# Score pass of a graph attention layer: the two edge products of a step on the two row halves of TensorE, each into a bank of its own, and the query products issued one step ahead

## The chip, the cores and the metric

The kernel runs on one core of one Trainium2 chip. The metric is the device time of one execution in microseconds. Every number of a profile below comes from one profiled execution of the kernel.

## The reference, cut to what matters

6250 nodes with 256 features go through a graph attention layer over 100,000 edges, a linear-attention block and a mixture of eight feed-forward experts. The change is in the score part of the graph attention (8 heads of 32 features):

```
k = (xn @ Wk.T + bk);  v = (xn @ Wv.T + bv);  q = (xn @ Wq.T + bq)
e = edge_attr @ We.T                      # 64 attributes -> 256, one row an edge
k_e = k[src] + e;  v_e = v[src] + e
alpha = einsum('ehc,ehc->eh', q[dst], k_e) / sqrt(32)
```

The softmax over the edges of each destination and the weighted sum of `v_e` come in later passes. The edges are sorted by destination.

## The kernel before, in words

The kernel has four stages in time: a pass over the nodes that makes the tables (to about 340 us), the **score pass** (about 340 to 1930 us), a value pass (about 2040 to 2580 us) and the expert stage (to the end). The change touches the score pass alone.

The score pass makes 450 steps (25 blocks `b` of `SB = 18`, `k = b * SB + s`). A step takes one pair of edge tiles, 2 x 125 edges, `w = 0, 1`, together with one tile of 125 nodes. The order on each engine is written out by hand and held together by semaphores:

- **SyncE** (SPq), for step `k`: loads two short rows for a later step (`load_ab`, L476), stores the finished value rows of step `k - 6` to `ve_d` (`store_ve`, L481) and loads the attributes of the 250 edges, transposed, into slot `s % 6` of the ring `att_b` (L502). A slot is free when `e_done` of six steps earlier is in. The attribute matrix `attr_t` lies in memory as 64 rows of 100,000 numbers.
- **GpSimd**, step `k`: two gathers (L625) fetch key and value rows (2 KB an edge) of 125 source nodes each into slot `s % 6` of `kg`, once the indices are copied (`idx_ready`) and the slot's last store has landed.
- **ScalarE**, step `k`: copies the indices (`start_edges`, L1060) and then makes the one-hot matrix `hott` from the spread destinations (`one_hot`, L1066 and L1067), in a ring of three.
- **TensorE**, step `k`: `qprod` (L762) for step `k - 5`, one-hot times the node tile's queries, two products into bank `2 + s % 2`; `eproj` (L746) for step `k - 5`, the edge product `attr @ We.T`, `w = 0` and `w = 1` into the two halves of bank `s % 2`; between the two, `spread` (L754) for step `k - 2`, a bf16 product on partitions 64 to 127, where `coef` and `ab_b` lie; and after these a piece of the linear-attention block (`mix`, L774 to L826; none to eight product pairs, by `mix_at`, `late_at`, `last_at`). The edge products stand on partitions 0 to 63, where `att_b` and `we` lie.
- **VectorE**, step `k`: `add_edges` (L1427) adds the edge product to keys and values of the gathered rows, `multiply` (L1435) multiplies the keys with the queries, `total` (L1441) sums over each head for step `k - 1`, `keep` (L1450) stores the sums for step `k - 2`; some steps carry a piece of the linear-attention block too.

`e_done`, `kv_added`, `q_done` and `mult_done` count the steps. `eproj` of step `k` waits until `kv_added` reaches `k - 1`, so the add of step `k - 2` has read the bank that is written again, and TensorE may be one edge product ahead. `qprod` waits in the same way for `mult_done`.

A product of fp32 operands shows as two passes in the trace: each has a weight load (PEld) and a matmul (PE), so that `eproj` has four matmul records a step.

## Time and profile before

| | |
|---|---|
| median of 3 runs | 3518.64 us (3511.38 to 3543.4) |
| profiled execution, its own time | 3552.69 us |
| its span, first to last instruction | 3550.9 us |
| mean granted TensorE clock in it | 0.961 of 2.4 GHz |
| step of the score pass, 600 to 1400 us | 226 steps in 800 us |

The span leaves out 1.8 us at the ends of the execution. The profiled execution is 34 us (1.0%) longer than the median of the runs. A busy share is the time in which an engine had an instruction in work; for DMA it is the mean over the core's 16 DMA engines of the time that their packets took.

### The profile page before, as it was taken

What the parts mean: (1) busy time and instruction counts of PE and PEld (TensorE: products, weight loads), DVE (VectorE), ACT (ScalarE), POOL (GpSimd) and SP (SyncE); (2) the same over time, 40 slices, a digit from 0 to 9 for tenths busy, and PEclk for the clock granted to TensorE, in tenths of its full rate; (3) what the DMA queues carried; (4) which work ended last, traced back from release to release, by engine and by line L of the source; (5) the groups of instructions that cost most, each with busy time, mean ns of one, the idle gap of its engine ahead of it and who ended that gap; (6) DMA issues with size and microseconds to landing.
All of it is one profiled execution on the core that took longest, in us unless ns stands there. A gap on an engine that the chain in (4) does not pass through costs nothing.

```text
span 3550.9 us, 72164 instructions
## 1 busy us (share of the span) xinstructions
PE 3186.8 (90%) x17312; PEld 2479.1 (70%) x17312; DVE 2793.7 (79%) x5687; ACT 1682.8 (47%) x4460; POOL 1646.0 (46%) x1803
## 2 busy tenths in 40 slices
PE   4997999999999999999999188888769999999999
PEld 3776666666666666666666155555569999999998
DVE  6775888888888888888887889999846666666665
ACT  1222333333333343333333256666546777777776
POOL 1223777777777777777775077777600000000000
PEclk9998899999999999999999599999979999999999
DMA  7345999899989899999998267777600000000000
GB/s 178 116 119 156 251 256 254 248 254 261 257 247 253 248 264 261 260 256 255 266 255 223 92 200 231 232 230 231 194 4 19 12 13 16 12 17 12 13 15 9
DMA packets 520909, 593.53 MB, mean 167 GB/s; under 512 B 187937, under 2 KB 396979, under 8 KB 520319
## 3 DMA queue, kind: packets, MB, share of 16 engines
q1 hardware_dynamic: 312408, 351.02, 34.0%
q0 software_dynamic: 201888, 232.77, 25.1%
q10 hardware_dynamic: 6409, 7.46, 0.7%
q8 instruction: 75, 1.23, 0.2%
q14 instruction: 129, 1.05, 0.1%
HBM read 426.91 MB, written 163.17 MB: 166 GB/s over the span
## 4 chain that ended last, share of the span: by engine, by line
PE 62%; DVE 12%; issue 8%; DMA 7%; SPq 3%; DVEq 3%; another core or an unknown queue 2%; ACT 1%; POOL 1%; ACTq 0%; POOLq 0%
PE psum L684 10%; PE psum L686 10%; PE psum L685 10%; PE psum L903 8%; PE psum L762 7%; PE psum L746 7%; PE psum L826 3%; DMA weights<-kv_tab,idx 3%; PE psum L817 2%; DVEq L1616 2%; DVE weights L1427 2%; DVE region_s L1613 1%; DVE part L1441 1%; DMA ve_d<-weights 1%
## 5 line engine op out<-in xcount | busy, mean ns | idle before, releaser
L625 POOL DMA_INDIRECT weights<-kv_tab,idx x450 | 549.1, 1220 | 254.5 <-issue 150.1
L762 PE MATMUL psum<-region_x,weights 125*125 x1800 | 493.3, 397 | 72.8 <-issue 39.7
L1183 ACT ACTIVATE region_s<-psum,bns 128x250 f32<-128x250 f32 x800 | 402.9, 554 | 287.8 <-PE psum L686 287.8
L746 PE MATMUL psum<-we,weights 64*125 64x256 f32 x1800 | 525.4, 410 | 0.0
L1665 DVE TENSOR_TENSOR parts_h<-region_s,parts_h 128x500 fp32r<-128x500 f32 x400 | 269.8, 679 | 311.2 <-ACT parts_h L1187 283.7
L903 PE MATMUL psum<-region_s 125*125 125x264 f32 x1800 | 452.5, 401 | 68.0 <-DVE region_s L1613 68.0
L1066 ACT ACTIVATE weights<-psum,region_s 125x250 f32<-125x250 f32 x450 | 211.3, 470 | 609.8 <-PE psum L754 289.0
L903 PEld LDWEIGHTS psum<-region_s 125*125 125x125 f32 x1800 | 304.6, 188 | 215.7 <-issue 76.9
L762 PEld LDWEIGHTS psum<-region_x,weights 125*125 125x125 f32 x1800 | 325.2, 191 | 177.3 <-issue 136.0
L625 POOL DMA_INDIRECT kv_more<-kv_tab,idx x300 | 370.4, 1235 | 126.9 <-issue 84.7
L746 PEld LDWEIGHTS psum<-we,weights 64*125 64x125 f32 x1800 | 298.5, 186 | 183.0 <-issue 155.2
L1427 DVE TENSOR_TENSOR weights<-weights,psum 125x1024 f32<-125x1024 f32 x225 | 274.1, 1218 | 82.7 <-remote 30.2
L1613 DVE TENSOR_TENSOR region_s<-region_s 125x512 f32<-125x512 f32 x450 | 308.5, 686 | 0.5 <-issue 0.5
L664 POOL TENSOR_SCALAR region_s<-iota,region_s 125x125 f32<-125x125 f32 x300 | 280.1, 944 | 14.7
L684 PE MATMUL psum<-parts_x,wx_up 128*128 128x250 f32 x800 | 233.9, 292 | 25.9 <-DVE wx_low L1657 25.9
L1187 ACT CAST parts_h<-region_s 128x500 fp32r<-128x500 f32 x400 | 244.2, 611 | 15.1
L817 PE MATMUL psum<-region_s,weights 128*128 128x250 f32 x800 | 225.8, 406 | 6.8 <-issue 2.9
L684 PE MATMUL psum<-wx_up,parts_h 128*125 128x256 f32 x800 | 226.8, 283 | 1.8 <-DVE region_s L1695 1.8
L1602 DVE TENSOR_TENSOR region_x<-region_x,psum 125x264 f32 x450 | 190.6, 423 | 46.9 <-issue 43.8
L686 PE MATMUL psum<-parts_x,wx_low 128*128 128x250 f32 x800 | 226.6, 283 | 0.0
L685 PE MATMUL psum<-parts_x,wx_up 128*128 128x250 f32 x800 | 226.3, 283 | 0.0
L686 PE MATMUL psum<-wx_up,parts_h 128*125 128x256 f32 x800 | 225.9, 282 | 0.0
(247 smaller groups left out, 7515.0 us busy)
## 6 DMA issues: line engine op xcount, KB each, us to landing
region_s<-ve_d SPq DMA_DIRECT2D x450, 256.0 KB, 3.0
ve_d<-weights SPq DMA_DIRECT2D x225, 256.0 KB
ve_d<-kv_more SPq DMA_DIRECT2D x150, 256.0 KB
weights<-in_attr_t SPq DMA_DIRECT2D x450, 62.5 KB
ve_d<-region_r SPq DMA_DIRECT2D x75, 256.0 KB
kv_tab<-region_s SPq DMA_DIRECT2D x50, 224.0 KB
region_s<-ab_d SPq DMA_DIRECT2D x450, 1.0 KB
weights<-kv_tab,idx POOLq DMA_INDIRECT x450
```

Source lines behind the costliest of these rows:

```text
L625: nc.gpsimd.indirect_dma_start(kg[r][0:T, w, :], None, kv_tab, bass.IndirectOffsetOnAxis(idx[:, r, w:w + 1], 0)).then_inc(gathered[r], 16)
L664: compared = nc.gpsimd.tensor_scalar(hot[:, s, w, :], iota[:, :], place_in[:, s, w:w + 1], None, ALU.is_equal)
L684: mm(to, lhs[0], rhs[0], start=start, stop=False)
L685: mm(to, lhs[0], rhs[1], start=False, stop=False)
L686: return mm(to, lhs[1], rhs[0], start=False, stop=stop)
L746: last = mm(psum[0:T, s % 2, w * D:(w + 1) * D], att_b[:, s % RP, w * T:(w + 1) * T], we[:, :], start=True, stop=True)
L762: last = mm(psum[0:T, 2 + s % 2, w * D:(w + 1) * D], hott[:, s % RA, w * T:(w + 1) * T], q_all[:, bass.ds(j, 1), :].rearrange("p o d -> p ...
L817: last = mm(psum[:, 5 if pair == 0 else 6, o * BN:(o + 1) * BN], wm1[:, c, n * 128:(n + 1) * 128], mx1t[:, c, :], start=(c == 0), stop=(c ...
L903: last = mm(bank, hot[:, s, w, :], pv[:, s, w, 0:PV], start=(w == 0), stop=(w == 1))
L1183: last = fn(fh[:, layer, o, :], psum[:, bk + e % 2, o * BN:(o + 1) * BN], ACT.Relu, bias=bns[:, layer, 1, col:col + 1], scale=bns[:, layer ...
L1427: tt(rows4, rows4, psum[0:T, s % 2, :].rearrange("p (w d) -> p w d", w=2).unsqueeze(2).broadcast_to((T, 2, 2, D)), ALU.add).then_inc(kv_ad ...
L1613: tt(pv[:, s, :, 0:D].rearrange("p w (h c) -> p w h c", h=H), vg[0:T, s].rearrange("p w (h c) -> p w h c", h=H), pv[:, s, :, D:PV].unsquee ...
```

## The change

What it does:

- `eproj` puts the two edge products of a step on different partitions: `w = 0` with attributes and weights on partitions 0 to 63, `w = 1` on 64 to 127. Each writes a bank of its own, 0 and 1, the same two in every step. It now waits until `kv_added` reaches `k`.
- `we` is held twice, once on each half of the partitions (one more constant load).
- The attribute load of a step writes 128 partitions of 125 numbers where it wrote 64 partitions of 250. Its source is walked as 2 x 64 x 125 (`w` outermost).
- `spread` goes behind both edge products, and its operands (`coef`, `ab_b`) move to partitions 0 to 63.
- `qprod` comes last of the three and is issued for step `k - 4`; the register that names its node tile is loaded one place further.

```
-        we = sb("we", [ED, D])
+        we = sb("we", [2 * ED, D])
-        ab_b = carve(8200, RP * E2 // 2).bitcast(BF16).rearrange("p (r n) -> p r n", r=RP)[64:128]
-        coef = weights[64:128, 1600:1600 + 64].bitcast(BF16)[:, 0:T]
+        ab_b = carve(8200, RP * E2 // 2).bitcast(BF16).rearrange("p (r n) -> p r n", r=RP)[0:64]
+        coef = weights[0:64, 1600:1600 + 64].bitcast(BF16)[:, 0:T]
-        att_b = weights[0:ED, 0:RP * E2].rearrange("p (r t) -> p r t", r=RP)
+        att_b = weights[:, 0:RP * T].rearrange("p (r t) -> p r t", r=RP)
-            sp.dma_start(we[:, :], a["w_e"]).then_inc(c_b, 16)
+            for w in range(2):
+                sp.dma_start(we[w * ED:(w + 1) * ED, :], a["w_e"]).then_inc(c_b, 16)
-                    sp.dma_start(att_b[:, s % RP, :], a["attr_t"][:, bass.ds(i * E2, E2)]).then_inc(att_in[s % RP], 16)
+                    sp.dma_start(att_b[:, s % RP, :], a["attr_t"][:, bass.ds(i * E2, E2)].rearrange("p (w t) -> w p t", w=2)).then_inc(att_in[s % RP], 16)
-            def eproj(k, s, turn_of, w):
-                if w == 0:
-                    pe.wait_ge(att_in[s % RP], turn_of * 16)
-                    wait(pe, kv_added, k - 1)
-                last = mm(psum[0:T, s % 2, w * D:(w + 1) * D], att_b[:, s % RP, w * T:(w + 1) * T], we[:, :], start=True, stop=True)
-                if w == 1:
-                    last.then_inc(e_done, 1)
+            def eproj(k, s, turn_of):
+                pe.wait_ge(att_in[s % RP], turn_of * 16)
+                wait(pe, kv_added, k)
+                for w in range(2):
+                    half = slice(w * ED, (w + 1) * ED)
+                    last = mm(psum[0:T, w, 0:D], att_b[half, s % RP, :], we[half, :], start=True, stop=True)
+                last.then_inc(e_done, 1)
...
-                        pe.load(regs, walk[0:1, 1, bass.ds(k, SU)])
-                    some = s >= LAGQ or not (isinstance(b, int) and b == 0)
-                    if some:
-                        qprod(k - LAGQ, (s - LAGQ) % SB, regs[s % SU])
-                        eproj(k - LAGQ, (s - LAGQ) % SB, b * (SB // RP) + (s - LAGQ) // RP + 1, 0)
+                        pe.load(regs, walk[0:1, 1, bass.ds(k + 1, SU)])
+                    if s >= LAGQ or not (isinstance(b, int) and b == 0):
+                        eproj(k - LAGQ, (s - LAGQ) % SB, b * (SB // RP) + (s - LAGQ) // RP + 1)
                     if s >= LAGS or not (isinstance(b, int) and b == 0):
                         spread(k - LAGS, (s - LAGS) % SB, b * (SB // RP) + (s - LAGS) // RP + 1)
-                    if some:
-                        eproj(k - LAGQ, (s - LAGQ) % SB, b * (SB // RP) + (s - LAGQ) // RP + 1, 1)
+                    if s >= LAGQ - 1 or not (isinstance(b, int) and b == 0):
+                        qprod(k - LAGQ + 1, (s - LAGQ + 1) % SB, regs[s % SU])
...
-                tt(rows4, rows4, psum[0:T, s % 2, :].rearrange("p (w d) -> p w d", w=2).unsqueeze(2).broadcast_to((T, 2, 2, D)),
+                tt(rows4, rows4, psum[0:T, 0:2, 0:D].unsqueeze(2).broadcast_to((T, 2, 2, D)),
```

## Rows read from the trace of the kernel before

**Rows 1.** The page: busy sums, the DMA share in 40 slices, the attribute load's row.

```profile
PE 3186.8 (90%) x17312; PEld 2479.1 (70%) x17312; DVE 2793.7 (79%) x5687; ACT 1682.8 (47%) x4460; POOL 1646.0 (46%) x1803
...
DMA  7345999899989899999998267777600000000000
...
weights<-in_attr_t SPq DMA_DIRECT2D x450, 62.5 KB
```

**Rows 2.** Busy time by stretch: us, PE, PEld, DVE, ACT, POOL, clock, DMA share, GB/s.

```profile
600.00:1400.00 800.00, 756.03 (x3237) 510.90 (x3236) 688.27 (x1205) 308.84 (x867) 578.92 (x501) 0.98 0.93 254
```

**Rows 3.** Groups of instructions with shapes, 600 to 1400 us.

```profile
L625 POOL DMA_INDIRECT weights<-kv_tab,idx x225 | 274.9, 1222 | 122.2 <-issue 70.1 <-ACT idx L1060 40.4 <-DMA ve_d<-weights 10.2
L746 PE MATMUL psum<-we,weights 64*125 64x256 f32 x902 | 262.4, 409 | 0.0
L762 PE MATMUL psum<-region_x,weights 125*125 x901 | 246.5, 396 | 35.7 <-issue 21.4 <-DVE weights L1435 6.8 <-DVE kv_more L1435 2.3
...
L1427 DVE TENSOR_TENSOR weights<-weights,psum 125x1024 f32<-125x1024 f32 x114 | 138.9, 1218 | 45.3 <-remote 15.8 <-DMA weights<-kv_tab,idx 11.0 <-PE psum L746 10.1
...
L754 PE MATMUL psum<-region_s,weights 64*125 64x250 bf16 x226 | 71.8, 318 | 8.3 <-issue 5.9 <-ACT weights L1067 2.0
```

**Rows 4.** Line L1427 (`add_edges`), 600 to 1400 us: its engine idle before it, until.

```profile
  remote: 23.8, 19
  PE psum L746: 14.3, 11
  issue: 12.4, 24
```

**Rows 5.** DMA queues and issues, 600 to 1400 us: packets, MB, share of 16 engines.

```profile
q0 software_dynamic: 101040, 115.99, 55.2%
q1 hardware_dynamic: 90519, 83.28, 35.7%
...
ve_d<-weights SPq DMA_DIRECT2D x114, 256.0 KB
ve_d<-kv_more SPq DMA_DIRECT2D x74, 256.0 KB
weights<-in_attr_t SPq DMA_DIRECT2D x226, 62.5 KB
ve_d<-region_r SPq DMA_DIRECT2D x38, 256.0 KB
region_s<-ab_d SPq DMA_DIRECT2D x226, 1.0 KB
region_s<-xnt_d SPq DMA_DIRECT2D x13, 250.0 KB
...
region_s<-skip_d SPq DMA_DIRECT2D x12, 224.0 KB
region_r<-xn_d SPq DMA_DIRECT2D x12, 224.0 KB
...
region_s<-skip_d SPq DMA_DIRECT2D x12, 26.0 KB
region_r<-xn_d SPq DMA_DIRECT2D x12, 26.0 KB
```

**Rows 6.** Timeline of TensorE in one step: start, length, what.

```profile
1013.44 0.48 PE L746 MATMUL psum<-we,weights 64*125 64x256 f32 x1
1013.45 0.32 PE L754 MATMUL psum<-region_s,weights 64*125 64x250 bf16 x1
1013.76 0.81 PE L746 MATMUL psum<-we,weights 64*125 64x256 f32 x3
```

**Rows 7.** Busy time by stretch: the load of the expert weights (SyncE's queue alone).

```profile
2000.00:2020.00 20.00, 0.00 (x0) 0.00 (x0) 19.96 (x2) 0.00 (x0) 0.00 (x0) 0.50 0.93 302
```

More of the change, by code:

```diff
@@ L337, in build @@
         f_stored = [sem(f"f_stored{u}") for u in range(2)]
-        CONST_A, CONST_B = 16 * 7, 16 * 9
+        CONST_A, CONST_B = 16 * 7, 16 * 10
         block = ctx.enter_context(nc.Block())
@@ L859, in _ @@
             each(NB, b_body)
-            pe.load(regs, walk[0:1, 1, STEPS:STEPS + SU])
+            pe.load(regs, walk[0:1, 1, STEPS + 1:STEPS + 1 + SU])
             for s in range(LAGQ):
-                qprod(STEPS - LAGQ + s, SB - LAGQ + s, regs[s])
-                eproj(STEPS - LAGQ + s, SB - LAGQ + s, (STEPS - LAGQ + s) // RP + 1, 0)
+                eproj(STEPS - LAGQ + s, SB - LAGQ + s, (STEPS - LAGQ + s) // RP + 1)
                 if s < LAGS:
                     spread(STEPS - LAGS + s, SB - LAGS + s, (STEPS - LAGS + s) // RP + 1)
-                eproj(STEPS - LAGQ + s, SB - LAGQ + s, (STEPS - LAGQ + s) // RP + 1, 1)
+                if s < LAGQ - 1:
+                    qprod(STEPS - LAGQ + 1 + s, SB - LAGQ + 1 + s, regs[s])
                 if s in last_at:
```

## The prediction

> **What bounds the kernel now.** I read the page first. TensorE has the largest busy sum, and the digits of the DMA engines stand at 8 and 9 in tenths through the score pass [rows 1]. The pass has 450 steps, one attribute load each [rows 1]. The table by stretch gives the middle of it: TensorE busy 756 of 800 us, VectorE 688, GpSimd 579, the DMA engines 0.93 at 254 GB/s, TensorE's clock 0.98 [rows 2]. With 226 steps in it a step takes 800 / 226 = 3.54 us. So four resources are within a few per cent of each other, and no one of them alone sets the step.
>
> TensorE's 95% are partly waiting time in disguise, since a record of a matmul overlaps the next: 902 records of L746 with 409 ns each would be 369 us, and they fill 262 [rows 3]. What the change wants to shorten is seen from the reader of the edge product: in front of `add_edges` VectorE waited 14.3 us for L746 in 226 steps, and 23.8 us for a releaser that the profile doesn't name [rows 4]. That is 0.06 and 0.11 us a step. The DMA engines have 7% left, 0.25 us a step. Whatever lets TensorE run faster can give no more than that before the transfers set the step.
>
> **The change, part by part.** *Edge products on two row halves.* Four passes of L746 a step. In the timeline three of them take 0.81 us, of which the last stands alone for 0.376, so a pass costs (0.81 - 0.376) / 2 = 0.22 us [rows 6] (0.376 is the median record of that line, the 0.48 of the first pass holds the wait for its weights). `spread` starts 0.01 us after the first pass, on the other half, and costs nothing now [rows 6]. If the halves run together, two passes remain in the time of four: 0.43 us less. `spread` then stands behind the edge products on the same half and must be paid: between nothing and its record of 0.32 us; I take half a pass, 0.11, as it has as many columns as a pass of L746 and only one pass. Net 0.1 to 0.4 us of TensorE's step, my value 0.3.
>
> Here a rule speaks against the change. In rows 6 `spread`, third in program order, ends at 1013.77, and the first pass of L746 at 1013.92: products on different row halves don't end in program order. The Trainium skill (TensorE: Matmul & The Clock Gate, Part 3) says that matmuls on different row groups overlap, but start and end strictly in program order. By that rule the second pass of `w = 0` would hold back the first of `w = 1`, three passes would remain, and TensorE would save 0.1 us. The trace doesn't agree with it. Neither value enters the sum below.
>
> *One pair of banks, `kv_added` up to `k`.* TensorE can't be a step ahead with the edge product any more. Behind the waiting `eproj` stand `spread`, on which ScalarE's one-hot waits and with it the indices and the gathers, `qprod` and the linear-attention piece. VectorE needs the next edge product only after multiply, total and keep, so the wait is covered while these last longer than `eproj`. If not, the cost is of the size of today's waits for L746: 0.06 us a step, 0.17 with the unnamed ones [rows 4], 30 to 80 us in all; the other bound is nothing. *`qprod` later and a step ahead:* its wait is for a product made a whole step before its use; nothing either way. *Constant load, register place:* once per kernel, nothing.
>
> *The attribute load.* This is the part that decides. It moves the same 62.5 KB [rows 5], but in 128 pieces of 500 B where there were 64 of 1000 B, and its source has the dimension of two outermost. How many DMA engines share a transfer can be counted. Each transfer gives one packet a row, and I assume one small closing packet for each engine that took part. In rows 5 the rows of the SyncE transfers are 226 x 256 stores, 226 x 64 attributes, 226 x 2 short rows, 13 x 256, and 24 x 250 for the last four: 82,100. The queue shows 90,519 packets, so 8,419 closed a transfer. With 16 engines for every one of the 739 transfers it would be 11,824; with two for the 226 two-row loads and 13 for the 24 loads of 26 KB (13 rows) it is 8,588, within 2% of the count. So a transfer is not spread over more engines than its outermost dimension gives, and I expect that of the new load: two engines, 64 pieces each, in every step, the same two.
>
> That the source's dimension counts, though the target has 128 partitions, no row shows: in every transfer of rows 5 the two sides have the same outermost size, or both a multiple of 16. The Trainium skill (DMA: Bandwidth & Descriptors, "Why a DMA increments its semaphore by 16 and not by 1") says that the engines are the largest number up to 16 that divides the slowest dimension of both sides, and its table of advice names an outermost dimension under 16 as what confines the whole transfer. The count in rows 5 agrees with it.
>
> The sum for one of these two engines, a step:
> - What it carries today: 0.93 x 3.54 = 3.29 us, less its sixteenth of the attribute load. The queue's 35.7% of 16 x 800 us are 4570 us for 83.28 MB, 18.2 GB/s [rows 5]; 64,000 B at that are 3.5 us, a sixteenth is 0.22. Leaves 3.07 us. Lower bound: all bytes, 254 GB/s x 800 us / 226 = 0.90 MB [rows 2] less 0.064, a sixteenth 52 KB, at the fastest rate that I found, 302 / 0.93 / 16 = 20.3 GB/s [rows 7]: 2.6 us.
> - Its half of the new load: 64 pieces of 500 B. By bytes at 18.2 GB/s 1.76 us; by packets, 4570 us / 90,519 = 50 ns each [rows 5], 3.2 us. I take 1.9, near the bytes, since the mean packet of that queue has 920 B.
> - Together 4.2 us (2.6 + 1.6 at 20.3 GB/s) to 6.3 us. My value: 2.8 for the old part, because the other fourteen engines will stand idle a third of the time and contend less, plus 1.9 is 4.7; at 96% use, little above today's 93%, 4.9 us.
>
> Gathers and stores need all sixteen engines to end, so the two slow ones set every step: nothing runs beside it to hide it. 450 x (4.9 - 3.54) = +612 us. Against the profiled execution that is 3552.7 + 612 = 4165 us; the median is 34 us below it, so **4130 us**. TensorE's 0.3 us drop out, as it waits. Its clock may fall in the pauses (it was 0.50 where TensorE had nothing to do, rows 7); a step's 756 / 226 = 3.35 us at full clock [rows 2] would be up to 6.7 at half, so stretches of it can add some tens of us.
>
> The bounds: 4.2 us a step gives 3519 + 450 x 0.66 = 3815; 6.3 gives 4760.
>
> **The rivals.**
> - *The load is spread over sixteen engines, and TensorE's gain comes through: faster.* For it: the target has 128 partitions, and rows 5 can't rule out that these count. Then TensorE saves 0.3 us, VectorE loses most of 0.17 us of waits [rows 4]; the DMA share caps the gain at 0.25 us. I take 0.1: 3519 - 45 = 3475 us. It decides from the point where the load's pieces cost no more than before. Against it: GpSimd's and the DMA's shares [rows 2, 3].
> - *Spread over sixteen, and nothing moves:* the transfers hold the step at 3.54 us, 3519 us, within 1%. The 500 B pieces by bytes cost what they did.
> - *Spread over sixteen, and the smaller pieces cost by the packet:* 64 more at 50 ns over 16 engines are 0.20 us a step at a share of 0.93: up to +90 us, with or without the single-bank wait (+30 to +80). 3580 us.
>
> **How the numbers follow.** Two engines 0.74, faster 0.10, unchanged 0.08, slightly slower 0.08. The likeliest case has its own range of 3815 to 4550; I give a tenth of it to more than 4550. To leave out no more than two in ten the range must reach down over the unchanged case, to 3490; above it ends at 4550. Faster by over 1%: 0.10. Within 1%, which is about what a measurement of this kernel can tell from no change: 0.09. Slower: 0.81.
>
> **What would show it.** In the changed profile a step of 4.9 us; the DMA share as a mean of 16 near 0.7 and under 200 GB/s in the score pass, though the pass is slower; q1's packets up by 64 a step for the attributes and down by 14 closing ones; L746 or `add_edges` waiting for the attribute load or for gathers, no longer for TensorE; TensorE's busy time well under 90% and a clock under 1 there. The stages behind unchanged. On TensorE the two halves' passes starting together would show the 0.43 us, three passes in a row the rule above. The prediction is wrong if q1 has 16 closing packets for each attribute load: then the step stays between 3.3 and 3.75 us and one of the rivals holds. It is wrong in size if the pieces of 500 B cost nearer 27 or nearer 50 ns than my 30.

## The result, and the profile after

The changed kernel is slower: 3822.38 us in the median of its runs (3812.48 to 3837.45), beside 3517.47 us of the kernel before on the same chip, ratio 1.0833 [1.0794, 1.0871]. The direction and the cause were forecast, the size was not: +305 us where +611 were expected. 3822 lies just above the 3815 us that the prediction worked out as its lowest value for a load on two engines. Two executions that ran far longer than the others of their kernel (5214 us with two loads a step, 17,334 us with `mix` ahead of `qprod`) are left out of the ratios below.

The profiled execution after took 3812.48 us (span 3810.7), 260 us more than the one of before (which was 35 us above its kernel's median, while this one is 10 below). Lines have moved: `load_ab` is L477 now, the store L482, the attribute load L503, `eproj` L748, `spread` L755, `qprod` L763, the add L1426, the one-hot L1065. The page of after, its busy sums, its slices, the chain by engine and the queue that carries the attribute load, to be laid beside [rows 1]:

```profile
PE 3134.9 (82%) x17312; PEld 2480.2 (65%) x17312; DVE 2800.9 (74%) x5687; ACT 1672.6 (44%) x4460; POOL 1642.3 (43%) x1803
...
DMA  7446777777778777777777736777740000000000
...
q1 hardware_dynamic: 334988, 351.06, 30.9%
...
PE 43%; SPq 17%; DMA 16%; DVE 11%; issue 7%; DVEq 3%; POOL 1%; ACT 1%; ACTq 0%; POOLq 0%
```

The 9s of the DMA line in the score pass have become 7s, and SyncE's queue and DMA transfers hold a third of the chain that ended last (the page of before has 3% and 7%). Nothing has taken TensorE's place as the longest busy sum; every engine simply waits more.

The table by stretch of after, its row to be read beside [rows 2]:

```profile
600.00:1400.00 800.00, 623.88 (x2802) 441.56 (x2803) 599.66 (x1047) 261.93 (x749) 497.39 (x433) 0.92 0.78 219
```

194 or 195 steps fit where 226 did: 4.11 us a step for 3.54. 450 x 0.57 = 257 us, so the steps of the score pass account for all of the 260 us between the two profiled executions.

DMA queues and issues of after in the same 800 us, beside [rows 5]:

```profile
q0 software_dynamic: 86951, 99.92, 47.8%
q1 hardware_dynamic: 87781, 71.78, 29.0%
...
ve_d<-weights SPq DMA_DIRECT2D x97, 256.0 KB
ve_d<-kv_more SPq DMA_DIRECT2D x64, 256.0 KB
weights<-in_attr_t SPq DMA_DIRECT2D x194, 62.5 KB
ve_d<-region_r SPq DMA_DIRECT2D x33, 256.0 KB
```

The count of packets says which way the load goes. The page of the kernel before has this line for q1:

```profile
q1 hardware_dynamic: 312408, 351.02, 34.0%
```

After has 334,988, 22,580 more. With 64 more data packets in each of 450 loads and 14 closing packets fewer (two engines take part, not sixteen) 450 x 50 = 22,500 are due; with sixteen engines it would be 28,800. So two engines carry the whole load. The other 80 packets are the second load of `we`: 64 rows and 16 closing packets. The closing packets can also be counted directly, as the records of 4 B in q1: 30,239 before and 23,955 after, 6284 fewer, which is 450 x 14 less those 16. In the 800 us of [rows 5] there are 8582 of them, beside the 8419 of the prediction's subtraction and the 8588 of its count with confined transfers.

The timeline of TensorE and of SyncE's queue in one step of after (start, length, what, idle time before it):

```profile
1003.16 0.70 PE L748 MATMUL psum<-we,weights 64*125 64x256 f32 x4 [0.99 <-issue]
1003.67 0.27 PE L755 MATMUL psum<-region_s,weights 64*125 64x250 bf16 x1
1003.98 1.12 PE L763 MATMUL psum<-region_x,weights 125*125 x4
1004.94 1.01 PE L818 MATMUL psum<-region_s,weights 128*128 128x250 f32 x4
1005.88 0.70 PE L748 MATMUL psum<-we,weights 64*125 64x256 f32 x4
```

```profile
1001.70 2.56 SPq L477 DMA_DIRECT2D region_s<-ab_d  x1
1004.31 0.61 SPq L482 DMA_DIRECT2D ve_d<-region_r  x1
1005.49 0.21 SPq L503 DMA_DIRECT2D weights<-in_attr_t  x1
1005.94 1.95 SPq L477 DMA_DIRECT2D region_s<-ab_d  x1
```

The four edge passes now take 0.70 us together; in [rows 6] the first starts at 1013.44 and the last ends at 1014.57, 1.13 us. Both values are the medians of 600 to 1400 us too. From the first edge pass to the start of what follows `spread` it was 1.06 us in the median before; here it is 0.73 where nothing delays what follows (the lower quartile), so that TensorE gains 0.33 us with `spread` paid. It had stood idle for 0.99 us ahead of them. The two-row load L477, two rows of 500 B, keeps SyncE's queue busy for about 2 us each time in this stretch. By the prediction's count it goes to two engines; that they are the same two, no record names. That line over 800 us in the kernel before (L476) and after (L477): number of issues, then minimum, median and maximum in ns:

```profile
L476 SPq DMA_DIRECT2D region_s<-ab_d x226: 3/246/1570, 600.4 to 1396.9; - x113
```

```profile
L477 SPq DMA_DIRECT2D region_s<-ab_d x195: 4/1390/6947, 598.9 to 1399.4; - x195
```

The waits of the other engines in after, 600 to 1400 us (total us, times, longest):

```profile
ACT weights L1065 <- PE psum L755: 273.7, 118, 5.5
...
PE psum L748 <- DVE weights L1426: 90.1, 58, 4.2
...
DVE weights L1426 <- DMA weights<-kv_tab,idx: 74.9, 38, 4.5
```

The add waits for gathers (11.0 us before for the same tile, [rows 3]), TensorE waits for the add, ScalarE for `spread`. Two suspects hold something up here: the two engines with the long load, and TensorE's new order with its stricter wait. The table does not tell cause from echo; that is what the experiments are for.

### The profile page after: what moved, and what is told of

Same layout as the page of the kernel before. It is cut to its first block, busy times and chain, and to the rows that moved or that the text cites. A ratio compares the mean times of both kernels' runs of the same rounds, so it can differ in the third digit from the quotient of the medians.

```text
span 3810.7 us, 72166 instructions
## 1 busy us (share of the span) xinstructions
PE 3134.9 (82%) x17312; PEld 2480.2 (65%) x17312; DVE 2800.9 (74%) x5687; ACT 1672.6 (44%) x4460; POOL 1642.3 (43%) x1803
## 3 DMA queue, kind: packets, MB, share of 16 engines
q1 hardware_dynamic: 334988, 351.06, 30.9%
## 4 chain that ended last, share of the span: by engine, by line
PE 43%; SPq 17%; DMA 16%; DVE 11%; issue 7%; DVEq 3%; POOL 1%; ACT 1%; ACTq 0%; POOLq 0%
PE psum L685 10%; PE psum L687 9%; PE psum L686 9%; PE psum L902 8%; SPq L477 6%; DMA weights<-kv_tab,idx 5%; DMA ve_d<-weights 5%; SPq L503 3%; DVE weights L1426 2%; SPq L482 2%; DVEq L1615 2%; DMA ve_d<-kv_more 2%; DMA region_r<-kv_tab,idx 2%; PE psum L763 2%; DMA ve_d<-region_r 1%
## 5 line engine op out<-in xcount | busy, mean ns | idle before, releaser
L748 PE MATMUL psum<-we,weights 64*125 64x256 f32 x1800 | 341.1, 453 | 382.0 <-DVE weights L1426 227.6
L1065 ACT ACTIVATE weights<-psum,region_s 125x250 f32<-125x250 f32 x450 | 211.0, 469 | 923.4 <-PE psum L755 654.5
L763 PE MATMUL psum<-region_x,weights 125*125 x1800 | 570.1, 444 | 25.3 <-DVE weights L1434 8.8
L748 PEld LDWEIGHTS psum<-we,weights 64*125 64x125 f32 x1800 | 150.8, 195 | 537.8 <-issue 537.2
L763 PEld LDWEIGHTS psum<-region_x,weights 125*125 125x125 f32 x1800 | 332.2, 205 | 212.3 <-issue 178.5
L1426 DVE TENSOR_TENSOR weights<-weights,psum 125x1024 f32<-125x1024 f32 x225 | 274.4, 1219 | 188.0 <-DMA weights<-kv_tab,idx 168.5
L685 PE MATMUL psum<-parts_x,wx_up 128*128 128x250 f32 x800 | 233.5, 292 | 25.8 <-DVE wx_low L1656 25.8
L1426 DVE TENSOR_TENSOR kv_more<-kv_more,psum 125x1024 f32<-125x1024 f32 x150 | 182.9, 1219 | 74.6 <-DMA kv_more<-kv_tab,idx 30.4
L626 POOL DMA_INDIRECT region_r<-kv_tab,idx x150 | 186.1, 1241 | 107.9 <-issue 98.2
L685 PE MATMUL psum<-wx_up,parts_h 128*125 128x256 f32 x800 | 226.7, 283 | 1.8 <-DVE region_s L1694 1.8
L687 PE MATMUL psum<-parts_h,wx_low 128*128 128x250 f32 x800 | 226.2, 283 | 0.0
```

The lines of the kernel that those rows point to most:

```text
L626: nc.gpsimd.indirect_dma_start(kg[r][0:T, w, :], None, kv_tab, bass.IndirectOffsetOnAxis(idx[:, r, w:w + 1], 0)).then_inc(gathered[r], 16)
L685: mm(to, lhs[0], rhs[0], start=start, stop=False)
L687: return mm(to, lhs[1], rhs[0], start=False, stop=stop)
L748: last = mm(psum[0:T, w, 0:D], att_b[half, s % RP, :], we[half, :], start=True, stop=True)
L763: last = mm(psum[0:T, 2 + s % 2, w * D:(w + 1) * D], hott[:, s % RA, w * T:(w + 1) * T], q_all[:, bass.ds(j, 1), :].rearrange("p o d -> p ...
L1426: tt(rows4, rows4, psum[0:T, 0:2, 0:D].unsqueeze(2).broadcast_to((T, 2, 2, D)), ALU.add).then_inc(kv_added, 1)
```

## The experiments

The theory: two DMA engines carry the load, and they set the step (A where the expectations use letters). Its rivals: pieces of 500 B cost more than pieces of 1000 B whatever the engines; TensorE's new order, or its wait for the add, costs the time (C); and later, that it is not the two engines' work but SyncE's queue, stuck behind them. All ratios are to the kernel before on the same chip, with 95% intervals.

**The change with the load on sixteen engines, by two DMAs.** Each half of the partitions gets its own load, whose outermost dimension is 64.

```
-    sp.dma_start(att_b[:, s % RP, :], a["attr_t"][:, bass.ds(i * E2, E2)].rearrange("p (w t) -> w p t", w=2))...
+    for w in range(2):
+        sp.dma_start(att_b[w * ED:(w + 1) * ED, s % RP, :], a["attr_t"][:, bass.ds(i * E2 + w * T, T)])...
-                pe.wait_ge(att_in[s % RP], turn_of * 16)
+                pe.wait_ge(att_in[s % RP], turn_of * 32)
```

> The changed kernel with its attribute load cut into two loads of 64 partitions each, so that the outermost dimension of both sides is 64 and all sixteen DMA engines share each; everything on TensorE stays as changed. Theory A, the two DMA engines that carry the attribute load set the step: the step falls from 4.11 to 3.4 to 3.6 us and the kernel to 3460 to 3560 us. Theory B, the single pair of banks with its wait for the add just made sets the step: nothing of that is touched, so 3780 to 3860 us. A value between would share the 305 us between them.

Measured: 3607.58 beside 3499.79 us, 1.0306 [1.0277, 1.0336]. Its row by stretch:

```profile
600.00:1400.00 800.00, 665.42 (x3141) 470.47 (x3141) 669.80 (x1168) 293.60 (x845) 563.79 (x488) 0.96 0.90 247
```

The larger part of the loss is gone, but 3% remain where none was expected: a miss. I read the rest as TensorE's, and tried three orders on this kernel. That was a detour, as the last runs show, for the remainder was mostly the second DMA itself.

**Only the engines, in the kernel before.** The source is walked so that the outermost dimension is 2 or 4, still 64 pieces of 1000 B; rows are permuted alike in `we`, so that the products are the same. TensorE's program is untouched.

```
-    sp.dma_start(we[:, :], a["w_e"])...
+    sp.dma_start(we[:, :], a["w_e"].rearrange("(r g) d -> g r d", g=2))...
-    sp.dma_start(att_b[:, s % RP, :], a["attr_t"][:, bass.ds(i * E2, E2)])...
+    sp.dma_start(att_b[:, s % RP, :], a["attr_t"][:, bass.ds(i * E2, E2)].rearrange("(r g) t -> g r t", g=2))...
```

> The kernel before, where only the source of the attribute load (and of the edge weights, in the same order of rows) is walked with a dimension of two outermost: the same 64 pieces of 1000 B on two DMA engines. Theory A: in the changed kernel the two engines carried 64 pieces at 0.029 us, 1.86 us of a step of 4.11, so 2.25 us for the rest; here 32 pieces at 0.046 us are 1.5 us, together 3.75 us a step, 3610 us (3580 to 3680). If the old load of an engine really costs the 2.8 us that I predicted with, 4.3 us a step and 3860 us. Theory B: TensorE is as before, 3500 to 3535 us.

Measured: 3730.56 us, 1.0659 [1.063, 1.0688], more than twice the loss that was expected.

```profile
600.00:1400.00 800.00, 723.04 (x2897) 487.96 (x2896) 620.32 (x1083) 280.54 (x774) 522.45 (x452) 0.91 0.82 229
```

203 loads fall in it, 3.94 us a step. With `g=4`:

> As the run with two engines, with a dimension of four outermost: 64 pieces of 1000 B on four DMA engines. Theory A: 16 pieces at 0.046 us are 0.74 us, plus 2.25 to 2.4 us is 3.0 to 3.15 us, under the step of 3.54: 3510 to 3550 us. If long packets count in full as I predicted (2.8 us and more), 3.55 to 3.8 us a step and 3530 to 3640 us. Theory B: 3500 to 3535 us.

Measured: 3522.81 us, 1.0084 [1.0055, 1.0113], 3.45 us a step. The closing packets of q1, 23,925 and 24,827 for the 30,239 of before, are 451 x 14 and 451 x 12 fewer (450 attribute loads and that of `we`): two engines, and four. So the number of engines alone makes 6.6 of the 8.3%, and four would have been nearly enough.

**Only the pieces, in the kernel before.** The two tiles of a ring slot lie one number apart, so that the one load has 128 pieces of 500 B on sixteen engines; the products read them where they lie.

```
-        att_b = weights[0:ED, 0:RP * E2].rearrange("p (r t) -> p r t", r=RP)
+        att_b = weights[0:ED, 0:RP * 2 * (T + 1)].rearrange("p (r w t) -> p r w t", r=RP, w=2)
-    sp.dma_start(att_b[:, s % RP, :], a["attr_t"][:, bass.ds(i * E2, E2)])...
+    sp.dma_start(att_b[:, s % RP, :, 0:T], a["attr_t"][:, bass.ds(i * E2, E2)].rearrange("p (w t) -> p w t", w=2))...
```

> The kernel before with the attribute ring spaced so that each row lands as two pieces of 500 B, on all sixteen engines as before; TensorE as before. If pieces cost by bytes: 3500 to 3535 us. If they cost by the packet (0.050 us each), 0.2 us a step: 3570 to 3620 us. Theory A and B both take the first. Beside the run with two loads it shows what TensorE's new order alone does.

Measured: 3507.86 us, 1.0027 [1.001, 1.0044]. The size of the pieces is next to free when sixteen engines share them.

**Only the stricter wait, in the kernel before.**

```
-                    wait(pe, kv_added, k - 1)
+                    wait(pe, kv_added, k)
```

> The kernel before with one number changed: eproj waits until kv_added reaches k instead of k - 1, so TensorE is never an edge product ahead; two banks as before. Of the 3.1% (108 us) that the changed kernel still loses with its load on sixteen engines. Theory C, the wait for the add costs them by holding back what is queued behind it on TensorE: here qprod is ahead of the wait, but the spread, the mix piece and the next step are behind it, and TensorE has no pace in reserve (four passes, not two), so 3570 to 3700 us. Theory D, the new order costs them (spread late, qprod late): 3490 to 3520 us here.

Measured: 3578.07 beside 3533.1 us, 1.0135 [1.0085, 1.0186].

**Only the order, in the kernel before.** Both edge products, `spread`, then `qprod` for step `k - 4`; banks and wait as before.

```
-                        pe.load(regs, walk[0:1, 1, bass.ds(k, SU)])
+                        pe.load(regs, walk[0:1, 1, bass.ds(k + 1, SU)])
-                        qprod(k - LAGQ, ...)
-                        eproj(k - LAGQ, ..., 0)
+                        for w in range(2):
+                            eproj(k - LAGQ, ..., w)
...
-                        eproj(k - LAGQ, ..., 1)
+                        qprod(k - LAGQ + 1, ...)
```

> The kernel before with the changed order alone: both edge products, then spread, then the query product of the next step; banks, row half and the wait for k - 1 as before. TensorE pays the spread in the open for its half a pass at most, since it still lies on the other half of the partitions. Theory C: 3490 to 3530 us. Theory D: 3560 to 3620 us.

Measured: 3613.73 us, 1.0249 [1.0202, 1.0296]. Among its waits, 600 to 1400 us:

```profile
PE psum L762 <- DVE weights L1436: 30.2, 26, 2.4
```

`qprod` (L762) for step `k - 4` needs the multiply (L1436) of step `k - 6`, where the old one needed that of `k - 7`. What TensorE issues behind it, `mix`, waits with it.

**Other orders with the two loads of the first run.** `spread` ahead of the edge products:

```
+                    spread(...)
                     eproj(...)
-                    spread(...)
                     qprod(k - LAGQ + 1, ...)
```

> The changed kernel with two loads of 64 partitions, and the spread moved ahead of the edge products, so that it isn't queued behind their wait for the add. Theory C: the one-hots, indices and gathers come earlier, ScalarE's wait for the spread (330 us in 600 to 1400) shrinks, part of the 3.1% comes back: 3520 to 3580 us. If the mix pieces and the query products behind the wait are what costs: 3590 to 3620 us, as with two loads. Theory D, in its part on the spread: the same as theory C.

Measured: 3629.73 us, 1.0286 [1.0237, 1.0334]: no help, a miss. The old order with `qprod` for step `k - 5` first, both edge products last:

```
+                    qprod(k - LAGQ, ...)
+                    spread(...)
                     eproj(...)
-                    spread(...)
-                    qprod(k - LAGQ + 1, ...)
```

> The changed kernel with two loads of 64 partitions, and the order of before: query product of the same step, spread, then the two edge products on their row halves, with the wait for kv_added k. The query product runs while VectorE makes the add for which the edge product waits. Theory C: only the mix piece stays behind the wait, and TensorE needs about 0.3 us less than before: 3460 to 3540 us. If the wait costs whatever is queued ahead of it: 3580 to 3620 us. Theory D: 3450 to 3510 us.

Measured: 3601.45 us, 1.0204 [1.0158, 1.025]. And that with the `mix` piece ahead of the edge products:

```
                     qprod(k - LAGQ, ...)
                     spread(...)
-                    eproj(...)
                     mix(...)
+                    eproj(...)
```

> The run with the old order (row halves, two loads), and on TensorE the linear-attention piece of the step moved ahead of the edge products: query product, spread, mix piece, edge products. Nothing but the next step is now queued behind the wait for the add. Theory C, what stands in TensorE's queue behind the wait is late and ScalarE and VectorE wait for it: VectorE's wait for the out-projection and ScalarE's for the hidden products fall back to before, and the kernel to 0.98 to 1.00 of before. If the coupling of TensorE and VectorE, one add to one edge product, costs by itself: 1.01 to 1.03, as with the old order. Worse than 1.03 if the edge product, now last, comes too late for the add.

Measured: 3586.42 beside 3500.58 us, 1.0261 [1.0222, 1.03]. No order went under 2%: whatever holds these kernels is not in TensorE's order. That made me look at what all of them share.

**Half of the load on two engines, in the kernel before.** Only the attributes of the first tile are loaded, 64 pieces of 500 B on two engines, and both products use them; the second tile's attributes are left out.

```
-    sp.dma_start(att_b[:, s % RP, :], a["attr_t"][:, bass.ds(i * E2, E2)])...
+    sp.dma_start(att_b[:, s % RP, 0:T], a["attr_t"][:, bass.ds(i * E2, T)].rearrange("(r g) t -> g r t", g=2))...
```

> The kernel before, with the attributes of the first edge tile alone loaded, on two DMA engines: 64 pieces of 500 B instead of 64 of 1000 B, and both edge products take them (the second tile's attributes are left out of the computation). Theory A, the time of the two engines: 32 pieces at 0.029 us are 0.93 us; with the run with whole rows on two engines (3.94 us a step less 32 x 0.046 to 0.052) the rest costs 2.3 to 2.5 us, together 3.2 to 3.4 us, at or under the step of before: ratio 0.98 to 1.01. If a transfer confined to two engines is slow for another reason, its issue in SyncE's queue or its closing, it is so at this size too: 1.04 to 1.07.

Measured: 3505.7 us, 1.0018 [1.0001, 1.0035]; the two-row load's issue has a median of 302 ns. 16 KB a step on each of two engines cost next to nothing here, in a kernel that also moves 32 KB a step less; the run with four engines has 16 KB on each of them and all of the bytes, at 0.8%.

**Two loads, in the kernel before**, as the partner of the first run.

```
-    sp.dma_start(att_b[:, s % RP, :], a["attr_t"][:, bass.ds(i * E2, E2)])...
+    for w in range(2):
+        sp.dma_start(att_b[:, s % RP, w * T:(w + 1) * T], a["attr_t"][:, bass.ds(i * E2 + w * T, T)])...
```

> The kernel before, with the attribute load of a step as two loads of 64 pieces of 500 B, one for each edge tile, as in the run of the changed kernel with two loads; TensorE as before. It prices the second issue in SyncE's queue (0.50 us a step): with the pieces alone the ratio was 1.003. I expect 1.00 to 1.01; if SyncE's queue with its 2 us a step holds back the stores, 1.01 to 1.03, and this part of the 3.1% isn't TensorE's.

Measured: 3582.11 us, 1.025 [1.0196, 1.0303]. The kernel was run once more, to read its profile:

> The kernel before with two attribute loads a step, once more, for a profile at full clock. If the 2.5% are real: ratio 1.015 to 1.035, a step of 3.5 to 3.65 us, and gathers that start later because the store in front of them in SyncE's queue is issued later. If they came from TensorE's clock in those runs: 1.00 to 1.01.

Measured: 3614.55 beside 3527.95 us, 1.0245 [1.0213, 1.0277]. What SyncE's queue waited for, first in the kernel before, then with two loads, 600 to 1400 us:

```profile
SPq L481 <- DVE kv_more L1427: 24.8, 24, 1.9
SPq L481 <- DVE weights L1427: 23.4, 20, 3.1
SPq L481 <- DVE region_r L1427: 22.8, 18, 1.9
```

```profile
SPq L481 <- DVE region_r L1428: 2.4, 5, 0.7
SPq L481 <- DVE kv_more L1428: 1.2, 4, 0.5
SPq L481 <- DVE weights L1428: 1.0, 4, 0.4
```

The store (L481) waits for the add that fills its rows: 71 us before, 4.6 us now. A queue that doesn't wait for its work comes late to it. The pieces of 500 B alone were 0.3%, and the DMA share is 0.92 in the same stretch, so I take the late queue for the cause of the rest. It is argued and not shown: the queue's recorded instructions fill 631 of the 800 us, for 539 before, and no run moved the second load to another queue. In the kernel before the second DMA costs 2.5%; in the changed one it is about 2% of the 3.1, by the run with one load on sixteen engines below.

**Only the order, `mix` ahead of `qprod`, in the kernel before.**

```
                        spread(...)
-                       qprod(k - LAGQ + 1, ...)
                        mix(...)
+                       qprod(k - LAGQ + 1, ...)
```

> The kernel with the changed order alone (ratio 1.025), and the linear-attention piece moved ahead of the query product of the next step: edge products, spread, mix piece, query product. The query product ahead waits for a multiply that comes a whole step later than the one it waited for before. Theory C': what was queued behind that wait, the mix piece, was the cost: ratio 0.995 to 1.01. If the wait itself, TensorE standing still with no step in reserve, costs: 1.015 to 1.03.

Measured: 3513.66 us, 1.0036 [1.0016, 1.0055], where the order without this move costs 2.5%. The price of the order was the work behind the wait, not the wait.

**The change with one load on sixteen engines.** The attributes lie in memory as a block of 128 x 125 for each pair of tiles, so that one DMA with outermost dimension 128 fills both halves.

```
-    sp.dma_start(att_b[:, s % RP, :], a["attr_t"][:, bass.ds(i * E2, E2)].rearrange("p (w t) -> w p t", w=2))...
+    sp.dma_start(att_b[:, s % RP, :], a["attr_t"][bass.ds(i, 1)].rearrange("o p t -> p (o t)"))...
-        "attr_t": g["edge_attr_64"].T,
+        "attr_t": np.ascontiguousarray(g["edge_attr_64"].reshape(EP, 2, T, ED).transpose(0, 1, 3, 2)).reshape(EP, 128, T),
```

> The changed kernel with the attributes laid out in memory as 400 blocks of 128 rows x 125 (row w * 64 + p), so that one load of 128 pieces of 500 B, one block of 64,000 B in a row, is shared by sixteen engines. TensorE as changed. Theory A, nearly all of the 305 us are the two engines and the second issue cost the 2.5%: ratio to before 0.99 to 1.02, by the quotient of the runs with two loads, 1.031 / 1.025 = 1.006. Theory C, the wait for the add and the order cost what they did alone (1.0135 and 1.025) less what the row halves give: 1.02 to 1.04.

Measured: 3569.81 beside 3529.93 us, 1.0111 [1.0076, 1.0145].

```profile
600.00:1400.00 800.00, 664.61 (x3219) 472.04 (x3217) 683.91 (x1196) 300.13 (x862) 578.08 (x501) 0.98 0.94 254
```

Its partner is the kernel before with blocks of 64 x 250 in memory:

```
+    sp.dma_start(att_b[:, s % RP, :], a["attr_t"][bass.ds(i, 1)].rearrange("o p t -> p (o t)"))...
+        "attr_t": np.ascontiguousarray(g["edge_attr_64"].reshape(EP, E2, ED).transpose(0, 2, 1)),
```

> The kernel before with its attributes laid out as 400 blocks of 64 rows x 250: the same 64 pieces of 1000 B on sixteen engines, read from one block of memory instead of from rows 400 KB apart. It is the partner of the run with one load on sixteen engines. The piece of 1000 B took 0.069 us in the mean and its median was 0.046; if the block is read without the long ones, 64 x 0.02 / 16 = 0.08 us a step less of DMA time: ratio 0.985 to 1.00.

Measured: 3537.13 us, 1.0019 [0.9998, 1.004]: the layout alone gives and costs nothing. So all of the change but its load costs 0.9%, and the load's two engines the other 7.

**Both repairs, and only the second.** The block load with `mix` ahead of `qprod`; then the change as it is, on two engines, with `mix` ahead. Both edits stand above.

> The run with one load on sixteen engines, with the linear-attention piece ahead of the query product of the next step. That move took 1.025 to 1.004 where the order alone was changed. Theory C': ratio to before 0.97 to 1.00, below the run with one load by 1 to 2%, since the wait for the query product is no longer paid and TensorE has two passes less. If the wait for the add is what binds: the same as the run with one load.

Measured: 3520.85 us, 0.997 [0.9953, 0.9988]: of all kernels here the only one below the kernel before, by a third of a per cent.

```profile
600.00:1400.00 800.00, 670.61 (x3320) 477.23 (x3320) 705.12 (x1238) 310.09 (x886) 596.65 (x514) 0.99 0.96 262
```

> The changed kernel as it is, attribute load on two engines, with the linear-attention piece ahead of the query product. Theory A, the two engines set the step and TensorE's order is hidden behind them: ratio 1.075 to 1.09, as the changed kernel (1.083). If both costs add: 1.06 to 1.07.

Measured: 3819.31 us, 1.0815 [1.0779, 1.0852]. TensorE's order repaired, the loss stays: behind two engines it is covered.

**The long load from another queue.** It could still be that the two engines had room, and that the time went because SyncE's queue stood still at L477 and issued the stores late. So the attribute load, still on two engines, goes to ScalarE's queue.

```
     # SyncE
-    i = sp.snap(regs[s % SU], min_val=0, max_val=EP - 1)
-    wait(sp, e_done, k - RP + 1)
-    sp.dma_start(att_b[:, s % RP, :], ...)
     # ScalarE, behind the copy of the indices
+    wait(act, e_done, k - RP + 1)
+    act.dma_start(att_b[:, s % RP, :], ...)
```

> The changed kernel with its attribute load, still on two engines, issued from ScalarE's queue behind the index copy of the same step instead of from SyncE's. Theory A1, the two engines are busy all the time and their time is the step: as the changed kernel, ratio 1.07 to 1.09. Theory A2, SyncE's queue is what is full, since its next issue to the same two engines waits until these have drained, and the store behind it, and with it the gathers, come late: the issue of the two-row load falls back to about 0.25 us, SyncE waits for adds again, and the step falls to 3.5 to 3.7 us, ratio 1.01 to 1.045, unless ScalarE now stands in the same way behind its own issues (then its index copies come late: 1.05 and more).

Measured: 3805.45 beside 3529.17 us, 1.0777 [1.0732, 1.0821]. Its row by stretch, and what SyncE's queue waited for:

```profile
600.00:1400.00 800.00, 621.48 (x2783) 436.71 (x2783) 596.02 (x1041) 258.85 (x742) 500.11 (x434) 0.91 0.79 220
```

```profile
SPq L477 <- PE psum L752: 191.0, 103, 8.6
SPq L482 <- DVE weights L1425: 75.7, 49, 3.5
SPq L482 <- DVE region_r L1425: 54.0, 31, 2.9
SPq L482 <- DVE kv_more L1425: 50.2, 49, 2.4
```

```profile
L1058 ACTq DMA_DIRECT2D weights<-in_attr_t x195: 514/929/8782, 599.9 to 1398.4; - x195
```

```profile
L477 SPq DMA_DIRECT2D region_s<-ab_d x194: 3/239/693, 603.0 to 1397.7; - x194
```

195 steps again, 4.10 us. SyncE's queue is now far ahead of its work: the stores wait 180 us for their adds, and even L477 waits 191 us for `spread` (L752). The time hardly moved. So SyncE's late stores alone don't set the step. The third fence, from the line of the load in this kernel (count, minimum, median and maximum in ns), shows that its issue can hold ScalarE's queue up to 8.8 us, with the copy of the indices behind it, the exception that the expectation named. What the other engines waited for (total us, times, longest):

```profile
PEld psum L745 <- DMA weights<-in_attr_t: 129.4, 51, 7.1
POOL weights L623 <- ACT idx L1056: 118.0, 43, 6.9
...
PE psum L745 <- DMA weights<-in_attr_t: 106.4, 44, 6.9
```

The gathers wait for the indices, which could be a held queue again. But TensorE stands 236 us for the attribute load itself (129.4 and 106.4), and that load's packets hardly ever pause: for 715 of the 800 us one of them starts within 0.3 us of the last. That speaks for the two engines. How much of the 4.10 us would be left if no engine's queue had to stand for the issue wasn't tried.

The fourth fence, L477 in this kernel, corrects a reading that lies near. The two-row load is issued in 0.24 us in the median here, 0.69 at most, though two engines carry as much as in after. So what held it there seems to be the backlog of its own queue, in which the attribute load went ahead of it, and not that the engines were full.

## Why the prediction was wrong in size and right in kind

**What held.** The load goes onto two engines, shown by the closing packets of after. That costs most of the loss: 6.6% with TensorE untouched (g=2), 0.8% with four engines, 0.3% for the smaller pieces on sixteen; and the change with its load on sixteen engines keeps 1.1%. Of the signs that were named, q1's packets, the waits for gathers and TensorE's busy time (78%) and clock (0.92) came; the step of 4.9 us and a rate under 200 GB/s did not (4.11 us, 219 GB/s). The Trainium skill (DMA: Bandwidth & Descriptors, "Why a DMA increments its semaphore by 16 and not by 1") takes the largest number up to 16 that divides the slowest dimension of both sides. After agrees with it for a source of 2 and a target of 128 partitions, the case that no row of before showed. The three rivals with sixteen engines, 0.26 together, fell with it.

**The step that failed** is the sum for one of the two engines, 2.8 us for what it carries today plus 1.9, over 96% use: 4.9 us where 4.11 were measured. The mis-sized term is the 2.8, with the 96% on top of it. The 1.9 was right: the 500 B packets of q1 in after were recorded at 29.0 ns in the mean (median 27), so 64 of them are 1.86 us. The other 2.25 of the 4.11 us are what was left for the rest. The 2.8 was drawn between 3.07, from the recorded time of the packets, and 2.6, from bytes at the fastest rate in [rows 7].

The kernel before had the right size in its own packet records, at their median and not at their mean: q0's packets of 4096 B took 159 ns in the median and 228 in the mean. With all packets of 600 to 1400 us but the attribute load's at the median of their size, an engine has 2.35 us a step; at the means it has 3.0. With the rest at the median and the load's packets at the mean that they had on their few engines, the sums are:

| kernel | rest | its share of the load | sum | measured step |
|---|---|---|---|---|
| after | 2.35 | 64 x 29.0 ns = 1.86 | 4.21 | 4.11 |
| two engines, g=2 | 2.35 | 32 x 51.7 ns = 1.65 | 4.00 | 3.94 |
| four engines, g=4 | 2.35 | 16 x 52.8 ns = 0.84 | 3.19 | 3.45, not set by them |

These are estimates from the packet records (the 51.7 and 52.8 hold a few 1000 B packets of other transfers), and they fit the first two steps within 2.5%. Bytes tell nearly the same, with another split between old and new (2.6 + 1.6 = 4.2). One of the two engines moves a sixteenth of everything else and half of the load (KB are 1000 B here):

- after: 219 GB/s x 4.11 us = 900 KB a step; (900 - 64) / 16 + 32 = 84 KB, 20.5 GB/s.
- g=2 in the kernel before: 229 x 3.94 = 902 KB, also 84 KB, 21.4 GB/s.
- load from ScalarE's queue: 220 x 4.10 = 902 KB, 84 KB, 20.6 GB/s.
- g=4: 262 x 3.45 = 904 KB; (904 - 64) / 16 + 16 = 68.5 KB, 19.9 GB/s.
- the kernel before: 254 x 3.54 = 899 KB, 56 KB, 15.9 GB/s.

So an engine here stops at 20.5 to 21.4 GB/s in the three kernels with 84 KB, close to the 20.3 that [rows 7] gave. At 20.3 84 KB need 4.1 us and hold the step; 68.5 KB need 3.4 and just fit under 3.45. By either sum four engines, or half of the load on two, cost next to nothing, and two engines with the whole load 7%.

The mean of the recorded packet time is not such a measure. In after the mean share of 0.78 is 0.78 x 16 x 4.11 = 51.3 us of engine time a step. If the two full engines hold 4.11 each of it, the other fourteen show 3.08 each for 52 KB, 17 GB/s. By those durations the full engines' 52 KB would leave 1.0 us for the new 32 KB. So a packet on an engine with room is recorded longer than it costs a full one. The load's own size of packet shows it: 1000 B took 69.2 ns in the mean on sixteen engines (before) and 51.7 on two (g=2), 500 B 38.3 on sixteen and 29.0 on two (after), with the same medians of 46 and 27. The 96% was wrong for the same reason: there was no slack to add.

**TensorE.** The halves do run together: four passes in 0.70 us, the 0.43 us less that were counted, and 0.33 us less with `spread`, where the prediction had 0.3. The Trainium skill (TensorE: Matmul & The Clock Gate, Part 3) has matmuls start and end in program order, from which the prediction worked out three passes in a row. After doesn't agree: in the median of 196 steps the four records start at 0, 0.01, 0.29 and 0.32 us, two pairs side by side. The ends of matmuls are modelled in the profile, so their order proves less than the starts; in [rows 6] too `spread` starts before the second pass of `w = 0`, which stands ahead of it in the program. That TensorE's gain "drops out" held on two engines: `mix` moved or not, 1.0815 or 1.0833. On sixteen 0.997 was the best, inside the 0.25 us a step that the prediction gave as the cap. That kernel still has the single pair of banks; what the row halves give without it was not run.

**The single-bank wait** was put at 0 to 80 us; alone it costs 1.35%, 48 us. Its size was right. That it is hidden behind the load in the change fits the sum, but was not run by itself.

**`qprod` later and a step ahead: "nothing either way"** was wrong. The order alone costs 2.5%, 88 us. I had looked at what `qprod`'s product is needed for and not at what it needs: for `k - 4` it waits for the multiply of `k - 6` instead of `k - 7`, and `mix` stood behind it. With `mix` ahead 0.4% remain. It is covered by the two engines in the change itself. With the load on sixteen, moving `mix` took 1.0111 to 0.997, so there it would have been the whole loss: the rival "slightly slower" on sixteen engines, 3580 us, had 0.08, and the block load measured 3570, though not by the mechanism that it named (the small pieces cost 0.3%).

**SyncE's queue** was not priced. In the change it is late behind the two-row load (1.39 us in the median for 0.25). That alone isn't what sets the step, as the load from ScalarE's queue showed. One DMA more for it to issue costs 2.5%. My first run of the change had both edits in one, and I read its 3.1% as TensorE's for the next three runs on it.

What is left of the sum: 6.6% (g=2) and 0.9% (the change on sixteen engines against its partner) make 7.5 of 8.3%. The rest, and the 0.17 us between the steps of g=2 and of after, are of the size of the pieces on full engines: 64 of 500 B are recorded at 1.86 us and 32 of 1000 B at 1.65. That was not run by itself.

## What to carry to other kernels

Before a DMA is reshaped, look at the outermost dimension of both sides, count the engines it leaves, and add up the work of one of these engines, by bytes against what a full engine moves or by packets at the median of their size; the mean share over sixteen hides two that are full, and a mean packet time holds waiting. An engine with room for the extra bytes takes them for under 1% here, and beyond that they lengthen the step. When one part of a change is undone by an edit that adds something of its own (here a second DMA), run the same edit in the old kernel too, and when a wait in an in-order queue moves, ask first what stands behind it.

## What the runs showed of the hardware

- DMA engines that carry half as many bytes again as before (84 KB a step for 56) stretched the step by 16% only: they had been running at 15.9 of some 20 to 21 GB/s at a recorded share of 0.93.
- A DMA issued behind a long load of its own queue on two engines holds that queue: two rows took 1.39 us in the median and up to 6.9 to issue, in place of 0.25. With the long load in ScalarE's queue the same issue took 0.24 us and 0.69 at most, at the same step of 4.1 us; there the long load's issue took up to 8.8.
- With the load's own packets as recorded on its two engines and all others at the median of their size, a full engine adds up to its step within 2.5% (4.21 for 4.11 us, 4.00 for 3.94); at the mean, an engine with room showed 3.0 us for what a full one did in about 2.25.
- One DMA more a step on SyncE's queue, 226 to 218 stores in 800 us, cost 2.5%, with the DMA engines' share at 0.92 for 0.93 and the same bytes a step.
- fp32 products on the two halves of the partitions ran in 0.70 us for four passes, starting in two pairs, 1.13 us on one half with `spread` beside them. What follows could start 0.33 us earlier.
